# Where the next layer's split weights are made: at the layer boundary with one set, or in mid-layer with two sets and the residual in DRAM

## The reference

```python
x = x + attn_first(layernorm(x))
```

```python
def ffn_stage(x):                      # x is layernorm(X1)
    for i in range(6):
        q, k, v = split(shift_tokens(x) @ Wqkv[i])      # 128 -> 3 * 1024
        q, k = l2norm(q) * q_scale[i], l2norm(k) * k_scale[i]
        q, k = rotary(q), rotary(k)                     # cos, sin and a position scale
        x = local_attention(q, k, v) @ Wo[i] + x
        h = layernorm(shift_tokens(x)) @ W1[i] + b1[i]
        x = (a(h) * gelu(gate(h))) @ W2[i] + b2[i] + x
    return x
X1 = x + first
out = X1 + ffn_stage(layernorm(X1))
```

## Time and profile before

| | |
|---|---|
| median of 3 runs | 3296.93 us (3294.43 to 3297.98) |
| the profiled execution | 3314.26 us, its span 3312.4 us |
| mean granted TensorE clock | 0.977 of full speed |
| busy: TensorE, its weight loads | 3145.3 us (95%), 2738.7 us (83%) |
| busy: VectorE, GpSimd, ScalarE | 2809.6 us (85%), 2622.3 us (79%), 2550.6 us (77%) |
| DMA | mean 39 GB/s, HBM read 19.17 MB |

### The profile page before, as it was taken

The page is one execution under the profiler, slowest core; times in us unless marked ns, Lnnn a source line. Parts: engine busy times, 40 slices in busy tenths (PEclk is TensorE's granted clock), DMA queues, the critical chain, the costliest instruction groups (busy, mean ns, idle before and its releaser), DMA issues.

```text
span 3312.4 us, 123078 instructions
## 1 busy us (share of the span) xinstructions
PE 3145.3 (95%) x52802; PEld 2738.7 (83%) x52802; DVE 2809.6 (85%) x3751; ACT 2550.6 (77%) x3699; POOL 2622.3 (79%) x2593
## 2 busy tenths in 40 slices
PE   7978999999999989999989999999999999999997
PEld 4647888888888878888878888888888888888886
DVE  7968888888888888888888888888888888888884
ACT  6756788777877878887878888878878777777875
POOL 6658888878878878888878888888888787878883
PEclk9989999999999999999999999999999999999997
DMA  2001111111211111121101111111111111111111
GB/s 65 2 10 37 60 38 37 34 34 41 64 37 34 41 32 42 37 63 35 41 28 47 37 58 40 34 34 43 40 58 40 33 35 39 38 34 34 41 34 37
DMA packets 57868, 129.81 MB, mean 39 GB/s; under 512 B 11120, under 2 KB 33264, under 8 KB 56560
## 3 DMA queue, kind: packets, MB, share of 16 engines
q1 hardware_dynamic: 57328, 121.94, 12.6%
HBM read 19.17 MB, written 2.10 MB: 6 GB/s over the span
## 4 chain that ended last, share of the span: by engine, by line
PE 90%; issue 4%; ACT 3%; POOL 2%; DVE 2%; DMA 0%; POOLq 0%; DVEq 0%; SPq 0%; ACTq 0%
PE pair L207 72%; PE pair L210 17%; POOL sq L395 0%; ACT qT L842 0%; ACT PT L823 0%; DVE wq_l L950 0%; DVE VB L317 0%; ACT sq L820 0%; ACT kT L859 0%; ACT oT L847 0%; POOL wq_l L950 0%; DVE qk L313 0%; ACT sq L832 0%; ACT VA L855 0%; ACT wq_h L920 0%
## 5 line engine op out<-in xcount | busy, mean ns | idle before, releaser
L1100 POOL TENSOR_TENSOR qk<-qk,ts 128x1024 f32<-128x1024 f32 x384 | 910.5, 2384 | 138.9 <-DVE ts L964 130.7
L1079 POOL TENSOR_TENSOR qk<-qk,rn 128x1024 f32<-128x1024 f32 x384 | 727.4, 1915 | 15.0
L960 DVE TENSOR_TENSOR qk<-pair,tab 128x1024 f32<-128x1024 f32 x384 | 468.5, 1220 | 271.4 <-ACT sq L820 265.8
L820 ACT ACTIVATE sq<-pair 128x1024 f32<-128x1024 f32 x192 | 197.0, 1026 | 455.4 <-PE pair L207 455.4
L207 PE MATMUL pair<-wq_h,xs_h 128*128 128x512 f32 x1154 | 516.4, 448 | 22.3 <-POOL xs_l L934 7.9
L1111 POOL TENSOR_TENSOR Sx<-Sx,rden 128x1024 f32<-128x1024 f32 x192 | 365.2, 1902 | 172.5 <-DVE rden L1026 172.5
L964 DVE TENSOR_TENSOR ts<-pair,tab 128x1024 f32<-128x1024 f32 x384 | 466.6, 1215 | 0.0
L207 PE MATMUL pair<-wq_h,xs_l 128*128 128x512 f32 x1152 | 465.1, 404 | 0.7 <-issue 0.6
L207 PE MATMUL pair<-wq_l,xs_h 128*128 128x512 f32 x1152 | 464.2, 403 | 0.3 <-issue 0.2
L968 DVE TENSOR_REDUCE ss<-sq 128x16 f32<-128x1024 f32 x384 | 464.2, 1209 | 0.0
L210 PEld LDWEIGHTS pair<-small,qk 128*128 128x128 f32 x3072 | 354.8, 144 | 84.2 <-issue 50.8
(11 more groups left out here) (127 smaller groups left out, 6711.8 us busy)
## 6 DMA issues: line engine op xcount, KB each, us to landing
VB<-VA SPq DMA_DIRECT2D x192, 384.0 KB, 3.5
VB<-VA SPq DMA_DIRECT2D x96, 128.0 KB, 3.4
wq_raw<-wqkv SPq DMA_DIRECT2D x6, 1536.0 KB, 8.5
xf<-xT SPq DMA_DIRECT2D x96, 64.0 KB, 1.9
xf<-xT SPq DMA_DIRECT2D x96, 63.8 KB, 2.0
wo_sb<-wo SPq DMA_DIRECT2D x6, 512.0 KB, 3.7
X<-x_in SPq DMA_DIRECT2D x4, 512.0 KB, 7.1
out<-X SPq DMA_DIRECT2D x16, 128.0 KB, 2.0
```

The lines of the kernel that those rows point to most:

```text
L820: A_.activation(sq[:, 0, :], one[:, :], ACT.Square).then_inc(S["squared"], 1)
L960: V_.tensor_tensor(h3(qk[:, now, kind, :], DH), h3(source[:, :], DH), rep(tab[:, 2 * kind, b, :], HEADS, DH), ALU.mult)
L1079: G_.tensor_tensor(x, x, bc(rn[:, then, kind * HEADS:(kind + 1) * HEADS], HEADS, DH), ALU.mult).then_inc(S["scaled"], 1)
L1100: G_.tensor_tensor(qk[:, now, kind, :], qk[:, now, kind, :], ts[:, kind, :], ALU.add).then_inc(S["added"], 1)
```

## The change

There are two sets, `wq_h`/`wq_l` and `wq_h2`/`wq_l2`, and `tab` has two halves; layer n uses set n % 2. So the next layer's set is made while this layer runs:

- SP loads one third of the raw weights at a time, at t = 12, 19 and 25, into `wq_raw`, which is now a third as large; the second and third load wait until the low part of the third before is made.
- ScalarE rounds the thirds at the end of t = 15, 21 and 27.
- GpSimd makes the low parts in halves of 512 columns at t = 16, 18, 22, 24, 28, 30, and the tables at t = 14 and 20 (two operations each), each between its add for q and its add for k. VectorE makes none any more.
- Layer 0's set is still made in the first stage, by thirds: rounding at its steps 3, 9, 15, low parts at 4, 10, 16.
- TensorE waits for the low parts at a layer's first block as before (the counts are doubled, since each third has two halves).

To find the room in SBUF, `X1` is given up after the first stage: as its tiles come ready it is written to DRAM (`x1_kept`, four stores of 512 KB), and `kT`, `oT` and `hid` of the layers lie in its place. `clear` therefore waits for the stores. In the last layer X1 comes back through the free `wq_raw`, which holds four sequences, each later one loaded when the sum four before it is done; the sums are written over `xT` and stored from there.

```diff
+        x1_kept = nc.dram_tensor("x1_kept", (P, TILES * DM), F32, kind="Internal").ap()
...
-        wq_raw = sb("wq_raw", [P, 3 * INNER])
+        wq_raw = sb("wq_raw", [P, INNER])
...
+        wq_h2 = sb("wq_h2", [P, 3 * INNER], F32R)
+        wq_l2 = sb("wq_l2", [P, 3 * INNER], F32R)
...
-        tab = sb("tab", [P, 4, BLOCKS, DH])
+        tab = sb("tab", [P, 2, 4, BLOCKS, DH])
...
-        kT = sb("kT", [P, PAIRS, WIN + LEN])
+        flat_x1 = X1[:, :, :].rearrange("p t c -> p (t c)")
+        KT = PAIRS * (WIN + LEN)
+        kT = flat_x1[:, 0:KT].rearrange("p (a k) -> p a k", a=PAIRS)
+        oT = flat_x1[:, KT:KT + INNER].rearrange("p (a q) -> p a q", a=PAIRS)
+        hid = flat_x1[:, KT + INNER:KT + INNER + 3 * LEN].rearrange("p (c q) -> p c q", c=3)
...
+        wq_high = (wq_h[:, :], wq_h2[:, :])
+        wq_low = (wq_l[:, :], wq_l2[:, :])
...
+        X1_RING = INNER // LEN
...
+        def x1_again(q):
...
+            at = q % X1_RING * LEN
+            return wq_raw[:, at:at + LEN].rearrange("p (b c) -> p b c", c=DM)
...
+        def out_rows(q):
...
+            return xT[:, q * LEN:(q + 1) * LEN].rearrange("p (b c) -> p b c", c=DM)
...
 
-            if 4 <= s < 7:
-                rest_of_projection(e, Place(e, 0).at(0), 0, s - 4, G_.tensor_tensor)
+            if s in (4, 10, 16):
+                for half in range(2):
+                    rest_of_projection(e, Place(e, 0).at(0), 0, s // 6, half)
...
-                tables(e, Place(e, 0).at(0), 0, G_.tensor_tensor)
+                for i in range(2):
+                    tables(e, Place(e, 0).at(0), 0, i)
...
 
-            if 3 <= s < 6:
-                e.wait_ge(S["wq_loaded"], 16)
-                round_projection(s - 3)
+            if s in (3, 9, 15):
+                e.wait_ge(S["wq_loaded"], 16 * (s // 6 + 1))
+                round_projection(0, s // 6)
...
-        def project(pair, high, low, first):
+        def project(layer, pair, high, low, first):
+            w_high, w_low = wq_high[layer % 2], wq_low[layer % 2]
-                mm(out, high, wq_h[:, cols], True, False)
-                mm(out, low, wq_h[:, cols], False, False)
-                last = mm(out, high, wq_l[:, cols], False, True)
+                mm(out, high, w_high[:, cols], True, False)
+                mm(out, low, w_high[:, cols], False, False)
+                last = mm(out, high, w_low[:, cols], False, True)
...
-                    e.wait_ge(S["wq_low_q"], layers(pl, 1, t // NBLOCKS, 1))
-                project(one, high, low, 0).then_inc(S["q_done"], 1)
+                    e.wait_ge(S["wq_low_q"], layers(pl, 2, t // NBLOCKS, 2))
+                project(layer, one, high, low, 0).then_inc(S["q_done"], 1)
...
                 round_x(e, pl, q)
-            if not pl.last and t == NBLOCKS - 1:
-                round_projections(e, pl, 1)
+            if not pl.last and t in ROUNDED_AT:
+                e.wait_ge(S["wq_loaded"], layers(pl, 48, 1, 16 * (ROUNDED_AT.index(t) + 1)))
+                round_projection(pl.turn + 1, ROUNDED_AT.index(t))
...
-        def round_projections(e, pl, ahead):
-            e.wait_ge(S["wq_loaded"], layers(pl, 16, ahead, 16))
-            for k, done in enumerate(("q_done", "k_done", "v_done")):
-                e.wait_ge(S[done], blocks(pl, done, 0, 1))
-                round_projection(k)
...
-        def round_projection(k):
+        LOADED_AT = (12, 19, 25)
+        ROUNDED_AT = (15, 21, 27)
+        LOW_AT = (16, 18, 22, 24, 28, 30)
+        TABLES_AT = (14, 20)
...
+        def round_projection(layer, k):
...
-            A_.activation(wq_h[:, part], wq_raw[:, part], ACT.Copy).then_inc(S["wq_high"], 1)
+            A_.activation(wq_high[layer % 2][:, part], wq_raw[:, :], ACT.Copy).then_inc(S["wq_high"], 1)
...
-        def tables(e, pl, ahead, tensor_tensor):
+        def tables(e, pl, ahead, i):
...
-            for i in range(2):
-                swapped = (qks[:, i, :].rearrange("p (o a c) -> p o a c", o=1, a=2)[:, :, ::-1, :]
-                           .broadcast_to([P, BLOCKS, 2, DH // 2]))
-                tensor_tensor(tab[:, 2 * i, :, :], rot[:, 2 * i, :, :], rep(qks[:, i, :], BLOCKS, DH), ALU.mult)
-                last = tensor_tensor(tab[:, 2 * i + 1, :, :].rearrange("p b (a c) -> p b a c", a=2),
-                                     rot[:, 2 * i + 1, :, :].rearrange("p b (a c) -> p b a c", a=2), swapped, ALU.mult)
-            last.then_inc(S["tabled"], 1)
...
-        def rest_of_projection(e, pl, ahead, k, tensor_tensor):
-            part = slice(k * INNER, (k + 1) * INNER)
+            to = tab[:, (pl.turn + ahead) % 2, :, :, :]
+            swapped = (qks[:, i, :].rearrange("p (o a c) -> p o a c", o=1, a=2)[:, :, ::-1, :]
+                       .broadcast_to([P, BLOCKS, 2, DH // 2]))
+            G_.tensor_tensor(to[:, 2 * i, :, :], rot[:, 2 * i, :, :], rep(qks[:, i, :], BLOCKS, DH),
+                             ALU.mult).then_inc(S["tabled"], 1)
+            G_.tensor_tensor(to[:, 2 * i + 1, :, :].rearrange("p b (a c) -> p b a c", a=2),
+                             rot[:, 2 * i + 1, :, :].rearrange("p b (a c) -> p b a c", a=2), swapped,
+                             ALU.mult).then_inc(S["tabled"], 1)
...
+        def rest_of_projection(e, pl, ahead, k, half):
...
+            layer = pl.turn + ahead
+            part = slice(k * INNER + half * UNIT, k * INNER + (half + 1) * UNIT)
...
-            tensor_tensor(wq_l[:, part], wq_raw[:, part], wq_h[:, part].bitcast(F32),
-                          ALU.subtract).then_inc(S["wq_low_" + "qkv"[k]], 1)
+            G_.tensor_tensor(wq_low[layer % 2][:, part], wq_raw[:, half * UNIT:(half + 1) * UNIT], wq_high[layer % 2][:, part].bitcast(F32),
+                             ALU.subtract).then_inc(S["wq_low_" + "qkv"[k]], 1)
...
             if pl.has(0):
-                if t == 0:
-                    e.wait_ge(S["tabled"], 1)
+                if t % NBLOCKS == 0:
+                    e.wait_ge(S["tabled"], layers(pl, 4, t // NBLOCKS, 4))
...
                 e.wait_ge(S["o_t"], q + 1)
-                new = X1[:, q * BLOCKS:(q + 1) * BLOCKS, :]
-                V_.tensor_tensor(new, new, h3(bank0[:, LEN:2 * LEN], P), ALU.add).then_inc(S["o_sum"], 1)
+                e.wait_ge(S["x1_back"], 16 * (1 + max(0, q - X1_RING + 1)))
+                V_.tensor_tensor(out_rows(q), x1_again(q), h3(bank0[:, LEN:2 * LEN], P), ALU.add).then_inc(S["o_sum"], 1)
...
                                             vec_b1[0:size, c:c + 1], hid[0:size, c, :], ALU.add, ALU.mult).then_inc(S["gated"], 1)
-            if not pl.last and t == NBLOCKS - 1:
-                for k in range(2):
-                    rest_of_projection(e, pl, 1, k, V_.tensor_tensor)
-                tables(e, pl, 1, V_.tensor_tensor)
...
                                      ALU.mult).then_inc(S["scaled"], 1)
-            if not pl.last and t == NBLOCKS:
-                rest_of_projection(e, pl, 1, 2, G_.tensor_tensor)
...
                     G_.tensor_tensor(qk[:, now, kind, :], qk[:, now, kind, :], ts[:, kind, :], ALU.add).then_inc(S["added"], 1)
+                    if kind == 0 and not pl.last and t in LOW_AT:
+                        rest_of_projection(e, pl, 1, LOW_AT.index(t) // 2, LOW_AT.index(t) % 2)
+                    if kind == 0 and not pl.last and t in TABLES_AT:
+                        tables(e, pl, 1, TABLES_AT.index(t))
...
+            if not pl.last and t in LOADED_AT:
+                k = LOADED_AT.index(t)
+                if k == 0:
+                    sp.wait_ge(S["wq_low_v"], layers(pl, 2, 0, 2))
+                else:
+                    sp.wait_ge(S["wq_low_" + "qk"[k - 1]], layers(pl, 2, 1, 2))
+                sp.dma_start(wq_raw[:, :], wqkv[turn + 1, :, k * INNER:(k + 1) * INNER]).then_inc(S["wq_loaded"], 16)
...
-                sp.wait_ge(S["wq_low_q"], layers(pl, 1, 0, 1))
-                sp.wait_ge(S["wq_low_k"], layers(pl, 1, 0, 1))
-                sp.wait_ge(S["wq_low_v"], layers(pl, 1, 0, 1))
-                sp.wait_ge(S["tabled"], layers(pl, 1, 0, 1))
+                sp.wait_ge(S["tabled"], layers(pl, 4, 0, 4))
...
-                apart(sp)
-                sp.dma_start(wq_raw[:, :], wqkv[turn + 1, :, :]).then_inc(S["wq_loaded"], 16)
...
+            if pl.last and t == DRAIN:
+                sp.wait_ge(S["wq_low_v"], layers(pl, 2, 0, 2))
+                sp.dma_start(wq_raw[:, :], x1_kept[:, 0:INNER]).then_inc(S["x1_back"], 16)
+            q = pl.seq(15)
+            if pl.last and q is not None and q + X1_RING < SEQS:
+                sp.wait_ge(S["o_sum"], q + 1)
+                ahead = q + X1_RING
+                sp.dma_start(wq_raw[:, q % X1_RING * LEN:(q % X1_RING + 1) * LEN],
+                             x1_kept[:, ahead * LEN:(ahead + 1) * LEN]).then_inc(S["x1_back"], 16)
...
 
+            dve.wait_ge(S["x1_stored"], 16 * 4)
...
-            sp.dma_start(wq_raw[:, :], wqkv[0, :, :]).then_inc(S["wq_loaded"], 16)
```

(9 more changed lines are left out.)

18 lines of the change are left out of this document (9 added, 9 removed).

## The result

| on one chip, medians | us | ratio to before, 95% interval |
|---|---|---|
| before | 3297.45 (3294.43 to 3317.86, 4 runs) | |
| after | 3255.34 (3251.20 to 3263.07, 4 runs) | 0.9862 [0.9817, 0.9907] |

A forecast was written before the change was run, and what follows sets the result against it. TensorE was taken to bound the kernel, on its path for 90% of the span. Terms -51.5 + 3.3 = -48.2 us took the median from 3296.93 to 3248.7 us, range 3240 to 3270.

The forecast's parts named there:

- Boundary work removed, 51.5: At the five layer boundaries, block 31 to block 1 falls to an ordinary pair's 30.17 us, gaining 51.5 us.
- Rival D: At the boundary another wait ends at the same time and the clock still falls; time within 0.2% of before; chance 0.03.
- What stays, 3.3: At the second and last boundaries, TensorE's short issue waits, partly hid by the long gap, return 3.3 us; bounds 0 and 6.
- The way to the 9 us of one boundary: At a boundary: TensorE idle 1.14 + 5.07 = 6.21 us, the other 2.8 put down to the slower clock.
- Half subtractions, 0: On GpSimd in mid-layer, 30 half subtractions of 1.28 us fit into its idle time and cost 0.
- The way of the cover: In GpSimd's even blocks, the second add comes 0.44 us late and the guard's 0.45 of idle time takes that up.
- The bound of 30 x 0.44: Upper bound for GpSimd's mid-layer half subtractions if the cover of 0.45 us is gone: 13 us.
- A: Rival, mid-layer: GpSimd's subtractions stretched by 0.93 us each, 0.92 beyond the cover, costing 28 us; time 3276; chance 0.09.
- Tables, roundings, loads, contention, 0: In mid-layer, GpSimd's tables (at most 9 us), ScalarE's roundings (at most 15), loads and SBUF contention each cost 0.
- First stage, 0 (-3 to +3): Pairs of halves may lengthen steps 10 and 16 by 1.6 us each; 5 and 6 give about as much back.
- Store of X, 0: After the first stage, the last 512 KB store lands in 3.7 us, within 4.97 before the clearing; cost 0.
- B's first part: At the clearing, a slow store holds the first stage by 3.5 us; the whole rival costs 6.7, chance 0.07.

The follow-up runs named there:

- after_again: The kernel after, with no edit, timed and profiled once more: median 3261.48 us, ratio 0.9879 to before.
- tables_at_boundary: Kernel after, but the tables made by VectorE at the end of step 31: median 3263.06 us, ratio 0.9881 to before.
- tables_only: Kernel before, with two halves of `tab` made by GpSimd in mid-layer, weights still at the boundary: median 3276.09 us, ratio 0.9912 to before.
- tables_first: Kernel before, with VectorE making the tables ahead of the two low parts, one set: median 3274.84 us, ratio 0.9884 to before.
- subtract_twice: Kernel after, with one extra subtraction into a spare tile ahead of each mid-layer half subtraction: median 3266.47 us, ratio 0.9873 to before.
- nothing_made: Kernel after, without mid-layer loads, roundings, subtractions and tables, output not the reference's: median 3262.51 us, ratio 0.9859 to before.
- stores_late: Kernel after, with all four stores of the residual held until its last tile: median 3263.48 us, ratio 0.9852 to before.

## Why the prediction was right, step by step

- *Boundary work removed, 51.5.* Right. Before's second profile has the same sum, and nothing else became late: the boundaries of after without issue waits take 30.16 to 30.17 us. Rival D fell with this.
- *What stays, 3.3.* Measured 3.8 and, in after_again, 4.1. At the second boundary two waits of 0.94 and 0.82 are in the rows, at the last 0.60 and 0.75. The prediction counted what the long gap hid, and it is back. (Its count of 41 such waits outside the boundaries holds with the two at the boundaries; without them there are 39.) The Trainium skill (Runtime: NRT & Kernel Launch, Instruction fetch mechanics) has the loading of the next block of code mostly hidden, by which nothing would have come back; whether these waits are that loading, no run here shows.
- *The way to the 9 us of one boundary.* The prediction listed idle times and the clock and gave no part a share. tables_at_boundary and tables_only show that the shares can't be added. tables_first shows the largest at the ordinary boundaries: tables beside GpSimd's scaling, stretched from 1.1 us to 4.3 (717.03 to the maxima at 721.32), and behind that the update of x, the wait of 5.07 and the low clock. The first two operations begin before the scaling or with it and take 0.35 and 0.28; the last two each end 0.14 us behind one of its two instructions. In before's timeline:

```profile
717.03 0.35 DVE L942 TENSOR_TENSOR tab<-rot,qks 128x128 f32<-128x128 f32 x1
717.30 0.28 DVE L943 TENSOR_TENSOR tab<-rot,qks 128x128 f32<-128x128 f32 x1
717.31 3.94 POOL L1079 TENSOR_TENSOR qk<-qk,rn 128x1024 f32<-128x1024 f32 x2
717.50 1.99 DVE L942 TENSOR_TENSOR tab<-rot,qks 128x128 f32<-128x128 f32 x1
719.41 1.98 DVE L943 TENSOR_TENSOR tab<-rot,qks 128x128 f32<-128x128 f32 x1
```

  The contention was in the rows, and the prediction read it only as a danger for mid-layer. tables_first both starts the tables earlier, in VectorE's wait for the rounding, and takes them out from beside the scaling; it doesn't part the two. How much of the 9 us is the lower clock, 2.8 us in the prediction, and how much idle time, no run measures by itself.
- *Half subtractions, 0.* Right. Estimated 1.28 us; GpSimd's source rows of after have 1289 ns in the median, and the adds of the same line are unstretched, 2384 against 2383:

```profile
L1123 POOL TENSOR_TENSOR qk<-qk,ts x384: 2347/2384/2427, 242.2 to 3187.7; 128x1024 f32<-128x1024 f32 x192
...
L977 POOL TENSOR_TENSOR wq_l<-wq_raw,wq_h x36: 1264/1289/1317, 29.1 to 2672.3; 128x512 fp32r<-128x512 f32 x36
```

- The way of the cover was told too narrowly. GpSimd's timeline of after in the block of rows 7:

```profile
974.04 2.39 POOL L1123 TENSOR_TENSOR qk<-qk,ts 128x1024 f32<-128x1024 f32 x1
976.38 1.30 POOL L977 TENSOR_TENSOR wq_l<-wq_raw,wq_h 128x512 fp32r<-128x512 f32 x1
977.62 2.41 POOL L1123 TENSOR_TENSOR qk<-qk,ts 128x1024 f32<-128x1024 f32 x1
980.12 0.29 POOL L1134 TENSOR_SCALAR ss<-ss 128x34 f32<-128x34 f32 x1
981.30 1.90 POOL L1138 TENSOR_TENSOR Sx<-Sx,rden 128x1024 f32<-128x1024 f32 x1 [0.89 <-DVE rden L1055]
```

  The idle times of 0.92 and 0.45 are gone as forecast (the second add comes 0.28 us later behind the first, 3.58 for 3.30, where 0.44 was forecast, and the guard no later), but another 0.89 follows before the weighing, and what lies behind has slack of its own: subtract_twice puts in 2.6 us where the prediction counted a cover of 1.37, and no step grows. The bound of 30 x 0.44 was too high for this reason; A, at 1.37 late for each, could not have cost its 28 us even if the stretching had come: subtract_twice puts in 1.3 more for each, where A has 0.93.
- *Tables, roundings, loads, contention, 0.* Right together: nothing_made leaves them all out and is no faster.
- *First stage, 0 (-3 to +3).* By ScalarE's squares of each tile (L451, now L472), steps 10 and 16 take 7.0 us for 5.8, 1.2 more each where 1.6 was reckoned; steps 5 and 6 give back 1.1 each, as the forecast had it; together +0.3. The start as a whole came 1.3 us later, in kernels with the same first stage 238.7 to 243.6 and in the two profiles of before 237.4 and 240.0, so the 1.3 isn't told from scatter.
- *Store of X, 0.* Right. A store of 512 KB landed in 2.7 us in the median (3.7 reckoned). B's first part, a clearing that waits on the store, comes only in stores_late.
- *The sum.* 48.2 forecast; 47.7 at the boundaries and 0.6 in the rest of the layers, less 1.3 at the start, make 47.0. The timed medians give 42.1 and 45.3, with runs of one program 4 to 31 us apart. That the profiled span came 7.6 below the forecast one is the 8.7 us of the clock in the last 80 us, a term that the prediction didn't have. And that the rest of the layers adds only 0.6 is luck within a scatter of 20 us; the forecast of the boundaries is borne out by their own rows, not by the total.

Not tried: a kernel with the clock held high at the boundary of before, which would part its 2.8 us from the idle time; and what makes the issue waits. Between 400 and 3200 us before has 39 waits over 0.6 us outside the boundaries (39.1 us), after 41 (42.3), so the change doesn't touch them. What sets where they fall, and with it which boundaries are dear, is open too.

## What to carry to other kernels

When several pieces stand at one place on an engine, look at what runs on the other engines beside each before moving them away: here one call moved two lines up gave 29.5 us at the boundaries, where a second set of weights, a round trip of the residual and new places for three buffers gave 47.7. Work on an engine that isn't the bound is free as long as what it delays is still ready when the bound wants it. GpSimd's idle time ahead of the guard, 1.37 us, was less than that slack, and making the added work two and three times measured it. VectorE's idle time, 3.4 us in a pair of steps, did not make an operation of 0.68 us free, as it ran beside GpSimd's. A part's price at a crowded place is not what is saved by taking it alone: take each away alone, and all together.

## What the runs showed of the hardware

- The stretch behind the last block's projection varies between 75.5 and 84.5 us with identical work, by TensorE's granted clock (0.97 and 0.80 of 2.4 GHz on average, part of it at 1.2), in kernels of both kinds. The difference is as large as the effect of one boundary, and it is in the span that one profile shows.
- VectorE's subtraction of 128x512 took 0.676 us alone and 1.49 beside a GpSimd instruction, its 128x128 product 0.277 and up to 2.42. GpSimd's own long ones keep their length in mid-layer (2347 to 2427 ns), but not where VectorE's stand ahead of them: its scaling, 1.91 us, took up to 2.88 in before and never over 1.92 in after, and its subtraction of 128x1024 3.32 for 2.39.
- A load of 512 KB landed in 5.6 us in the median, three in place of one of 1536 KB in 8.5; other loads of 512 KB (`wo_sb`) landed in 3.5.
- The step behind a rounding of the projection's weights by ScalarE (16, 22, 28) is 0.15 us shorter than its like, 15.22 for 15.38, and in before and nothing_made, which have no such roundings there, it is 15.37 to 15.39. Step 10, behind the rounding of the feed-forward weights, is 15.22 in all kernels. TensorE has no idle time in either kind of step, and I have no cause for it.
